# Other rows leave early: the gate's row split at 416, and a last output tile in two steps

## The chip, the cores and the metric

One NeuronCore of a Trainium2 chip. The metric is the device time of one execution in microseconds, the median of three runs. Times within the profile are in us from the start of its span, unless marked ns.

## The reference

Cross-attention with a gate, for 8 batches of 100 query rows (800 rows in all, d = 1024) over 722 memory rows of 512:

```python
memory_proj = einsum('bme,de->bmd', memory, W_mem)
scores = einsum('bnd,bmd->bnm', hidden, memory_proj) / sqrt(D)
memory_context = einsum('bnm,bmd->bnd', softmax(scores), memory_proj)
gate = sigmoid(einsum('bnf,df->bnd', concat([hidden, memory_context]), W_gate) + b_gate)
fused = hidden + gate * memory_context
out = fused * rsqrt(mean(square(fused), -1) + 1e-6) * norm_w
```

All in float32. The kernel keeps the precision by splitting each operand of a large matmul into a high and a low part in float32r and adding three products (high by high, low by high, high by low).

## The kernel before

Everything up to the memory context is done for all 800 rows in the first 217 us and is not touched here. What is left is the half of the gate that comes from the memory context, and the end: gate, fusion, mean of squares, scaling, output. Data lies transposed: a tile t of the output is 128 of the 1024 features on the partitions, with the 800 rows along the free dimension, so one matmul streams rows as columns.

**Steps.** A step (t, r0, r1) of the list `STEPS` (L32) makes output tile t for rows r0 to r1. The rows are parted at `FIRST` = 512 (L20): "early" rows 0 to 511 and "late" rows 512 to 799 (288 of them). The order is written by hand: tiles 0 and 1 early, tile 0 late, tiles 2 to 7 early (the last of these is step `END0` = 8), then tiles 1 to 7 late (steps 9 to 15, `LAST` = 15). Step n uses PSUM bank 4 or 5 in turn (`gate_bank`, L126).

**TensorE.** `gate_mc(n)` (L451) runs 8 tiles of the contraction by 3 products, 24 matmuls (L294) whose moving operand has r1 - r0 columns, each with a weight load of 128 columns. Inside step 10 it makes the means of squares for the early rows (`mean_first`, L466: a matmul with the square sums as weights and one column that holds 1/1024), and inside step 11 it spreads the inverse roots over the partitions (`inverse`, L474: ones times a diagonal matrix).

**ScalarE**, for each step (L707 to L716): the weight split for a later step, `sigmoid(n)` (L675) from PSUM, `seed(n + 2)` (L686), which puts the saved half of the gate into the bank of step n + 2, and `finish(n - 1)` (L696), which is a square and then `weigh` (L691), a scaling by norm_w. At two steps, 9 and 15, finish comes ahead of the sigmoid. For the last step VectorE squares (L932), and ScalarE only weighs (L718).

**VectorE**, for each step: `gate_times` (L877), `fuse` (L883), `sum_squares(n - 1)` (L864), and from step 11 on two scaled outputs of the early rows (`output`, L895). **SyncE** stores the early rows in transposed form, two tiles at a time (L278), as these become ready.

**The late rows leave otherwise**: TensorE transposes them back, in three chunks of `CHUNK` = 96 rows. Behind the last gate step TensorE does, in program order (L500 to L514): the first seven tiles of chunks 0 and 1 turned, a wait for the square sums and the last square, the late means (two matmuls for each chunk, L506 and L507), the last tile of chunks 0 and 1, and all of chunk 2. VectorE adds eps to the three means (L934), GpSimd raises them to -0.5 (L954), and then each chunk is scaled by its roots on its way out of PSUM: ScalarE takes the left half of its 1024 columns (L722), VectorE the right half (L938). SyncE stores a chunk as 96 rows of 4 KB (L282) when both halves are there, and waits for all stores (L284). `TURN` (L23) says which two PSUM banks a chunk is turned into.

Of the kernel before, what the change touches and what calls it, by code (L numbers as in the profile page):

```python
# [7 lines left out]
P = 128  # L8
R = B * N
H = R // 2  # L10
KD, KC = D // P, C // P
# [3 lines left out]
BANK = 512  # L15
WB = KD * P
EPS = 1e-6
WARM_UP = 27

FIRST, CHUNK = 512, 96  # L20
ROWS2 = (R - FIRST) // CHUNK

TURN = ((0, 1), (2, 7), (4, 3))  # L23


J_MEM = 0
# [3 lines left out]


STEPS = [(0, 0, FIRST), (1, 0, FIRST), (0, FIRST, R)] + [(t, 0, FIRST) for t in range(2, KD)] \  # L32
    + [(t, FIRST, R) for t in range(1, KD)]
LAST = len(STEPS) - 1

END0 = STEPS.index((KD - 1, 0, FIRST))
# [5 lines left out]
def build(nc, xT, ctxT, ctxN, w_mem, w_gate_x, w_mem_t, w_gate_mc, b_gate, norm_w, outT, out_rows):  # L42
    F32, F32R = mybir.dt.float32, mybir.dt.float32r
    ALU, ACT, AX = mybir.AluOpType, mybir.ActivationFunctionType, mybir.AxisListType

    top = ExitStack()
    with top:  # L47
        def sb(scope, name, shape, dt=F32):
            return scope.enter_context(nc.sbuf_tensor(name, shape, dt))
# [11 lines left out]
        acc = sb(top, "acc", [P, KD, R])  # L61
# [34 lines left out]
        minus_half = sb(top, "minus_half", [P, FIRST // P])  # L96
        rms = sb(top, "rms", [P, FIRST // P])
        rms_late = sb(top, "rms_late", [CHUNK, ROWS2])
        rms_diag = sb(top, "rms_diag", [P, FIRST // P, P])


        w_hi.append(sb(top, "w_hi2", [P, WB], F32R))
# [11 lines left out]
        def bank(i, cols, rows=P, at=0):  # L114
            return ps[0:rows, i * BANK + at:i * BANK + at + cols]
# [5 lines left out]
        G2B, RIB = 4, 3  # L121

        def late_mean(i, n=1):
            return bank(6, n, CHUNK, 8 + i)

        def gate_bank(n):  # L126
            r0, r1 = STEPS[n][1:]
# [160 lines left out]
        def _(pe):  # L288
# [162 lines left out]
            def gate_mc(n, after=None, work=None):  # L451

                t, r0, r1 = STEPS[n]
                pe.wait_ge(w_lo_done, J_G2 + 1 + t)
                if n >= 2:
                    pe.wait_ge(seeded, n - 1)
                for k in range(KD):
                    if n == 0:
                        pe.wait_ge(mc_lo_done, k + 1)
                    done = three([gate_bank(n)], w_tile(W_HOME[t], k), [(act_hi[:, k, r0:r1], act_lo[:, k, r0:r1])],  # L460
                                 k == 0 and n < 2, k == KD - 1, onto=n >= 2)
                    if k == after:
                        work()
                done.then_inc(gate_made, 1)

            def mean_first():  # L466

                pe.wait_ge(summed, END0 + 1)
                for i in range(FIRST // P):
                    done = nc.tensor.matmul(bank(6, 1, P, i), square_sum[:, i * P:(i + 1) * P], mean_w[:, :],  # L470
                                            start=True, stop=True)
                done.then_inc(mean_made, 1)

            def inverse():  # L474

                pe.wait_ge(diag_done, FIRST // P)
                for i in range(FIRST // P):
                    done = nc.tensor.matmul(bank(RIB, P, P, i * P), ones[:, :], rms_diag[:, i, :],  # L478
                                            start=True, stop=True)
                done.then_inc(inv_made, 1)  # L480

            def late_sums(i):
                at = FIRST + i * CHUNK
                return square_sum[:, at:at + CHUNK]

            def turn(i, t0, t1):

                at = FIRST + i * CHUNK
                for t in range(t0, t1):
                    done = nc.tensor.transpose(bank(TURN[i][t // 4], P, CHUNK, t % 4 * P), acc[:, t, at:at + CHUNK],  # L490
                                               ident[:, :])
                return done
# [4 lines left out]
            gate_mc(END0 + 3, 4, inverse)  # L497
            for n in range(END0 + 4, LAST + 1):
                gate_mc(n)
            pe.wait_ge(weighted, LAST)  # L500
            turn(0, 0, KD - 1)
            turn(1, 0, KD - 1)
            pe.wait_ge(summed, LAST)
            pe.wait_ge(late_squared, 1)
            for i in range(ROWS2):
                nc.tensor.matmul(late_mean(i), late_sums(i), mean_w[:, :], start=True, stop=False)  # L506
                done = nc.tensor.matmul(late_mean(i), square[:, LAST % 2, i * CHUNK:(i + 1) * CHUNK], mean_w[:, :],  # L507
                                        start=False, stop=True)
            done.then_inc(late_mean_made, 1)
            pe.wait_ge(weighted, LAST + 1)  # L510
            turn(0, KD - 1, KD).then_inc(turned, 1)
            turn(1, KD - 1, KD).then_inc(turned, 1)
            pe.wait_ge(out_done, KD)
            turn(2, 0, KD).then_inc(turned, 1)  # L514


# [1 line left out]
        def _(act):  # L518
# [188 lines left out]
            for n in range(LAST + 1):  # L707
                if n in SPLIT_AT:
                    split_gate_w(SPLIT_AT[n])
                if n == END0 + 1 or n == LAST:  # L710
                    finish(n - 1)
                sigmoid(n)
                if n + 2 <= LAST:
                    seed(n + 2)
                if n > 0 and n not in (END0 + 1, LAST):
                    finish(n - 1)  # L716
            act.wait_ge(late_squared, 1)
            weigh(LAST)  # L718
            for i in range(ROWS2):
                act.wait_ge(late_rooted, 1)  # L720
                act.wait_ge(turned, i + 1)
                nc.scalar.activation(row_out[:, i * D:i * D + BANK], bank(TURN[i][0], BANK, CHUNK), ACT.Copy,  # L722
                                     scale=rms_late[:, i:i + 1]).then_inc(row_left, 1)
# [3 lines left out]
        def _(dve):  # L727
# [160 lines left out]

            def diagonals():
                dve.wait_ge(rooted, 1)  # L890
                for i in range(FIRST // P):
                    nc.vector.tensor_scalar(rms_diag[:, i, :], ident[:, :], rms[:, i:i + 1], None,
                                            ALU.mult).then_inc(diag_done, 1)

            def output(k):  # L895
# [15 lines left out]
            gate_times(END0 + 1)  # L911
            fuse(END0 + 1)
            dve.wait_ge(mean_made, 1)
            nc.vector.tensor_scalar(rms[:, :], bank(6, FIRST // P), EPS, None, ALU.add).then_inc(mean_copied, 1)
            diagonals()
            done = 0
            for n in range(END0 + 2, LAST):
# [6 lines left out]
                while done < min(KD, 2 * (n - END0 - 2)):  # L924
                    output(done)
                    done += 1
            sum_squares(LAST - 1)
            gate_times(LAST)
            fuse(LAST)
            part = acc[:, KD - 1, FIRST:R]  # L930
            dve.wait_ge(fused, LAST + 1)
            nc.vector.tensor_tensor(square[:, LAST % 2, 0:R - FIRST], part, part, ALU.mult).then_inc(late_squared, 1)  # L932
            dve.wait_ge(late_mean_made, 1)
            nc.vector.tensor_scalar(rms_late[:, :], late_mean(0, ROWS2), EPS, None, ALU.add).then_inc(mean_copied, 1)  # L934
            for i in range(ROWS2):
                dve.wait_ge(late_rooted, 1)
                dve.wait_ge(turned, i + 1)
                nc.vector.tensor_scalar(row_out[:, i * D + BANK:(i + 1) * D], bank(TURN[i][1], BANK, CHUNK),  # L938
                                        rms_late[:, i:i + 1], None, ALU.mult).then_inc(row_right, 1)


        @block.gpsimd
        def _(pool):
            nc.gpsimd.memset(ident[:, :], 0.0).then_inc(ident_zeroed, 1)
            pool.wait_ge(ident_zeroed, 1)
# [6 lines left out]
            nc.gpsimd.tensor_tensor(rms[:, :], rms[:, :], minus_half[:, :], ALU.pow).then_inc(rooted, 1)  # L952
            pool.wait_ge(mean_copied, 2)
            nc.gpsimd.tensor_tensor(rms_late[:, :], rms_late[:, :], minus_half[0:CHUNK, 0:ROWS2],  # L954
                                    ALU.pow).then_inc(late_rooted, 1)


# [28 lines left out]
```

## Time and profile before

| | |
|---|---|
| median of 3 runs | 303.08 us (302.94 to 303.28) |
| the profiled execution | 303.27 us |
| its span | 301.5 us |
| granted TensorE clock, mean | 0.992 |
| TensorE busy | 97% of the span |
| VectorE, ScalarE busy | 55%, 52% |
| HBM read, written | 42.80 MB, 3.28 MB |

The profile is of one execution. A busy time counts the instructions of an engine from start to end. Matmuls overlap one another, so the pace of a row of matmuls is read from the starts of the first and the last, and not from the length of one. The weight loads (PEld) run beside the matmuls (PE). A chain of waits goes back from the last instruction, at each step to what released it. A line's number is that of the kernel above.

### The profile page before, as it was taken

The numbers are of one execution on the slowest core, as the hardware profiler recorded it, in microseconds if no ns is written. First come the engines' busy times: TensorE is split into PE (matmuls) and PEld (weight loads), VectorE is DVE, ScalarE is ACT, GpSimd is POOL, SyncE is SP. The second block draws the span as 40 slices with busy tenths as digits, with TensorE's granted clock in tenths as the row PEclk, the third lists the DMA queues.
The fourth block names the chain that finished last, engine by engine and source line by source line (L and its number), as shares of the span: only waits on it lengthen the run. The fifth ranks groups of instructions, "written<-read, shape, count | busy, mean of one in ns | idle before, by whom it ended". The sixth has DMA issues, their size and how long they took to land.

```text
span 301.5 us, 4214 instructions
## 1 busy us (share of the span) xinstructions
PE 292.5 (97%) x1647; PEld 272.2 (90%) x1647; DVE 166.5 (55%) x236; ACT 157.4 (52%) x231; POOL 2.6 (1%) x8
## 2 busy tenths in 40 slices
PE   8999999999999999999999999999999999999990
PEld 7999999898999989899898989999988888899980
DVE  2757564557575666756566534432365753444862
ACT  4648246464573836448373616454356845454542
POOL 0000000000000000000000000000000000001000
PEclk9999999999999999999999999999999999999996
DMA  6997291733928367372944011095123400000335
GB/s 208 408 385 244 94 339 56 238 115 111 277 89 316 136 199 262 105 257 102 299 161 150 13 70 40 29 340 236 70 72 136 143 2 0 1 0 2 139 141 157
DMA packets 18351, 46.29 MB, mean 154 GB/s; under 512 B 1520, under 2 KB 2288, under 8 KB 18336
## 3 DMA queue, kind: packets, MB, share of 16 engines
q1 hardware_dynamic: 18336, 46.09, 44.4%
q8 instruction: 10, 0.16, 0.2%
q14 instruction: 5, 0.04, 0.1%
HBM read 42.80 MB, written 3.28 MB: 153 GB/s over the span
## 4 chain that ended last, share of the span: by engine, by line
PE 96%; DMA 1%; DVE 1%; ACT 0%; DVEq 0%; issue 0%; ACTq 0%
PE ps L294 69%; PE ps L406 11%; PE ps L382 11%; PE ps L396 1%; PE ps L413 1%; DMA acc<-xT 1%; PE ps L319 0%; DVEq L47 0%; PE ps L490 0%; PE ps L322 0%; PE ps L325 0%; PE ps L478 0%; PE ps L470 0%; DVE x_again L938 0%; PE ps L506 0%
## 5 line engine op out<-in xcount | busy, mean ns | idle before, releaser
L294 PE MATMUL ps<-act_hi,w_hi 128*128 128x400 f32 (+2 forms) x268 | 79.4, 347 | 0.0
L294 PE MATMUL ps<-act_hi,w_lo 128*128 128x400 f32 (+2 forms) x268 | 78.7, 344 | 0.0
L294 PE MATMUL ps<-act_lo,w_hi 128*128 128x400 f32 (+2 forms) x268 | 78.7, 344 | 0.0
L294 PEld LDWEIGHTS ps<-act_hi,w_hi 128*128 128x128 f32 x268 | 49.2, 188 | 2.9
L294 PEld LDWEIGHTS ps<-act_lo,w_hi 128*128 128x128 f32 x268 | 49.8, 188 | 1.8
L294 PEld LDWEIGHTS ps<-act_hi,w_lo 128*128 128x128 f32 x268 | 49.8, 188 | 1.8
L729 DVE TENSOR_TENSOR w_lo<-w_stage,w_hi 128x1024 fp32r<-128x1024 f32 (+2 forms) x23 | 26.0, 1131 | 23.4 <-ACT w_hi L526 22.2
L729 DVE TENSOR_TENSOR cn_lo<-cn_stage,cn_hi 128x1536 fp32r<-128x1536 f32 (+2 forms) x24 | 28.5, 1217 | 5.2 <-ACT cn_hi L545 5.2
L729 DVE TENSOR_TENSOR ct_lo<-ct_stage,ct_hi 128x1444 fp32r<-128x1444 f32 x16 | 25.8, 1654 | 0.5 <-ACT ct_hi L537 0.5
L526 ACT ACTIVATE w_hi<-w_stage 128x1024 fp32r<-128x1024 f32 x20 | 21.0, 1054 | 7.9 <-PE ps L294 6.1
L621 ACT ACTIVATE pc<-ps,row_inv 100x512 f32<-100x512 f32 x8 | 5.5, 688 | 34.1 <-PE ps L406 34.1
L537 ACT ACTIVATE ct_hi<-ct_stage 128x1444 fp32r<-128x1444 f32 x16 | 21.7, 1409 | 0.0
L382 PE MATMUL ps<-ct_hi,qb_hi 128*100 128x362 f32 x64 | 21.4, 334 | 0.0
L605 ACT ACTIVATE probs<-ps,neg_top 100x722 f32<-100x722 f32 x8 | 6.9, 866 | 27.2 <-DVE neg_top L807 27.2
L382 PE MATMUL ps<-ct_hi,qb_lo 128*100 128x362 f32 x64 | 21.0, 328 | 0.0
L382 PE MATMUL ps<-ct_lo,qb_hi 128*100 128x362 f32 x64 | 21.0, 328 | 0.0
L683 ACT ACTIVATE gate<-ps,bias_t 128x288 f32<-128x288 f32 (+1 forms) x14 | 8.1, 579 | 24.2 <-PE ps L294 24.2
L881 DVE TENSOR_TENSOR gate<-gate,mc 128x512 f32<-128x512 f32 (+1 forms) x16 | 9.2, 573 | 20.0 <-ACT gate L683 20.0
L729 DVE TENSOR_TENSOR act_lo<-mc,act_hi 128x800 fp32r<-128x800 f32 x8 | 7.9, 993 | 20.5 <-ACT mc L654 20.5
L406 PE MATMUL ps<-cn_hi,pt_hi 128*100 128x512 f32 (+1 forms) x48 | 18.9, 394 | 0.0
L406 PE MATMUL ps<-cn_hi,pt_lo 128*100 128x512 f32 (+1 forms) x48 | 18.9, 393 | 0.0
L406 PE MATMUL ps<-cn_lo,pt_hi 128*100 128x512 f32 (+1 forms) x48 | 18.9, 393 | 0.0
(99 smaller groups left out, 447.1 us busy)
## 6 DMA issues: line engine op xcount, KB each, us to landing
ct_stage<-ctxT SPq DMA_DIRECT2D x16, 722.0 KB, 9.2
cn_stage<-ctxN SPq DMA_DIRECT2D x8, 768.0 KB, 5.4
cn_stage<-ctxN SPq DMA_DIRECT2D x8, 512.0 KB
w_stage<-w_gate_x SPq DMA_DIRECT2D x8, 512.0 KB, 7.9
w_stage<-w_gate_mc SPq DMA_DIRECT2D x8, 512.0 KB, 3.6
x_again<-xT SPq DMA_DIRECT2D x1, 3200.0 KB, 13.0
acc<-xT SPq DMA_DIRECT2D x6, 400.0 KB, 7.3
w_stage<-w_mem_t SPq DMA_DIRECT2D x4, 512.0 KB, 5.5
```

The lines of the kernel that those rows point to most:

```text
L294: done = nc.tensor.matmul(o, wgt, stream[h][part], start=first and wgt is wh and part == 0, stop=last and wgt is wl, skip_group_check=onto)
L382: done = nc.tensor.matmul(bank(h, MH + 1, N), lhs[:, k, :], rhs[:, k, at:at + MH + 1], start=k == 0 and part == 0, stop=k == KC - 1 and pa ...
L396: done = nc.tensor.transpose(o, probs[:, t * P:t * P + rows], ident[0:N, 0:N])
L406: done = nc.tensor.matmul(bank(PCB, C, N), lhs[0:rows, t, :], rhs[0:rows, t, :], start=t == 0 and part == 0, stop=t == MT and part == 2)
L413: done = nc.tensor.transpose(bank(PTB5, N, P, c * N), pc[:, c * P:(c + 1) * P], ident[0:N, 0:N])
L526: nc.scalar.activation(w_hi[home][:, :], w_stage[:, slot, :], ACT.Copy).then_inc(w_hi_done, 1)
L537: nc.scalar.activation(ct_hi[:, 2 * s:2 * s + 2, :], ct_stage[:, 2 * s:2 * s + 2, :], ACT.Copy).then_inc(ct_hi_done, 1)
L605: nc.scalar.activation(probs[:, :].rearrange("p (h m) -> p h m", h=2), scores, ACT.Exp, bias=neg_top[:, :], scale=float(D) ** -0.5, accum_ ...
L621: nc.scalar.activation(pc[:, :], bank(PCB, C, N), ACT.Copy, scale=row_inv[:, :]).then_inc(pc_scaled, 1)
L683: nc.scalar.activation(part, part if n < 2 else gate_bank(n), ACT.Sigmoid, bias=bias_t[:, t:t + 1]).then_inc(gate_done, 1)
L729: return nc.vector.tensor_tensor(out, whole, hi.bitcast(F32), ALU.subtract)
L881: nc.vector.tensor_tensor(part, part, mc[:, t, r0:r1], ALU.mult).then_inc(gated, 1)
```

## The change

- The rows are parted at 416: 416 early rows, 384 late ones, in three chunks of 128 rows.
- The last output tile's late rows are two steps: 256 rows (416 to 671, chunks 0 and 1), then 128 (672 to 799, chunk 2). There are 17 steps, and `LAST` is 16.
- The means of chunks 0 and 1 no longer need the last step: TensorE makes them right behind it, from the square sums alone, and VectorE adds eps to them between `gate_times(16)` and `fuse(16)`; GpSimd has a power of its own for them. The mean of chunk 2 comes later and goes to another bank (7).
- TensorE's order behind the last step: means of chunks 0 and 1, all of chunk 0 turned, mean of chunk 2, chunk 1 turned, chunk 2 turned.
- VectorE's order: eps of chunk 2, then the right halves of chunks 0, 1 and 2.
- ScalarE puts the finish ahead of the sigmoid at steps 9, 15 and 16.
- The matrices of the early rows' scaling are 104 by 104, four of them, in place of 128 by 128.

```diff
-FIRST, CHUNK = 512, 96
-ROWS2 = (R - FIRST) // CHUNK
-
-TURN = ((0, 1), (2, 7), (4, 3))
+FIRST, CHUNK = 416, 128
+ROWS2, LATE = (R - FIRST) // CHUNK, R - CHUNK
+FC = FIRST // 4
+
+TURN = ((0, 1), (2, 3), (5, 4))
...
-    + [(t, FIRST, R) for t in range(1, KD)]
+    + [(t, FIRST, R) for t in range(1, KD - 1)] + [(KD - 1, FIRST, LATE), (KD - 1, LATE, R)]
...
         def late_mean(i, n=1):
-            return bank(6, n, CHUNK, 8 + i)
+            return bank(6, n, CHUNK, 8 + i) if i < ROWS2 - 1 else bank(7, n, CHUNK, BANK - 1)
...
             for n in range(END0 + 4, LAST + 1):
                 gate_mc(n)
+            pe.wait_ge(summed, LAST)
+            for i in range(ROWS2 - 1):
+                done = nc.tensor.matmul(late_mean(i), late_sums(i), mean_w[:, :], start=True, stop=True)
+            done.then_inc(late_mean_made, 1)
             pe.wait_ge(weighted, LAST)
-            turn(0, 0, KD - 1)
-            turn(1, 0, KD - 1)
-            pe.wait_ge(summed, LAST)
+            turn(0, 0, KD).then_inc(turned, 1)
             pe.wait_ge(late_squared, 1)
-            for i in range(ROWS2):
-                nc.tensor.matmul(late_mean(i), late_sums(i), mean_w[:, :], start=True, stop=False)
-                done = nc.tensor.matmul(late_mean(i), square[:, LAST % 2, i * CHUNK:(i + 1) * CHUNK], mean_w[:, :],
-                                        start=False, stop=True)
-            done.then_inc(late_mean_made, 1)
+            nc.tensor.matmul(late_mean(ROWS2 - 1), late_sums(ROWS2 - 1), mean_w[:, :], start=True, stop=False)
+            nc.tensor.matmul(late_mean(ROWS2 - 1), square[:, LAST % 2, 0:CHUNK], mean_w[:, :],
+                             start=False, stop=True).then_inc(late_mean_made, 1)
+            pe.wait_ge(out_done, KD)
+            turn(1, 0, KD).then_inc(turned, 1)
             pe.wait_ge(weighted, LAST + 1)
-            turn(0, KD - 1, KD).then_inc(turned, 1)
-            turn(1, KD - 1, KD).then_inc(turned, 1)
-            pe.wait_ge(out_done, KD)
             turn(2, 0, KD).then_inc(turned, 1)
...
-                if n == END0 + 1 or n == LAST:
+                early = n == END0 + 1 or n >= LAST - 1
+                if early:
                     finish(n - 1)
                 sigmoid(n)
...
             for i in range(ROWS2):
-                act.wait_ge(late_rooted, 1)
+                act.wait_ge(late_rooted, 1 + (i == ROWS2 - 1))
...
+            def late_mean_plus_eps(late, at, n):
+                dve.wait_ge(late_mean_made, late + 1)
+                nc.vector.tensor_scalar(rms_late[:, at:at + n], late_mean(at, n), EPS, None,
+                                        ALU.add).then_inc(mean_copied, 1)
+
             gate_times(LAST)
+            late_mean_plus_eps(0, 0, ROWS2 - 1)
             fuse(LAST)
...
-            nc.vector.tensor_scalar(rms_late[:, :], late_mean(0, ROWS2), EPS, None, ALU.add).then_inc(mean_copied, 1)
-            for i in range(ROWS2):
-                dve.wait_ge(late_rooted, 1)
+            def right_half(i):
+                dve.wait_ge(late_rooted, 1 + (i == ROWS2 - 1))
                 dve.wait_ge(turned, i + 1)
...
+            late_mean_plus_eps(1, ROWS2 - 1, 1)
+            for i in range(ROWS2):
+                right_half(i)
...
-            pool.wait_ge(mean_copied, 2)
-            nc.gpsimd.tensor_tensor(rms_late[:, :], rms_late[:, :], minus_half[0:CHUNK, 0:ROWS2],
-                                    ALU.pow).then_inc(late_rooted, 1)
+            for late, at, n in ((0, 0, ROWS2 - 1), (1, ROWS2 - 1, 1)):
+                pool.wait_ge(mean_copied, late + 2)
+                part = rms_late[:, at:at + n]
+                nc.gpsimd.tensor_tensor(part, part, minus_half[0:CHUNK, 0:n], ALU.pow).then_inc(late_rooted, 1)
```

## Rows read from the trace of the kernel before

**Rows 1.** The page, busy us of each engine, share of the span, instructions

```profile
PE 292.5 (97%) x1647; PEld 272.2 (90%) x1647; DVE 166.5 (55%) x236; ACT 157.4 (52%) x231; POOL 2.6 (1%) x8
```

**Rows 2.** Stretches: length, busy us (matmuls) of each engine, clock, DMA share, GB/s

```profile
182.80:217.65 34.85, 34.85 (x196) 34.85 (x194) 13.69 (x17) 17.14 (x22) 0.00 (x0) 1.00 0.41 155
232.11:265.50 33.39, 33.39 (x146) 27.00 (x145) 16.76 (x24) 18.73 (x29) 0.00 (x0) 1.00 0.14 46
276.04:289.77 13.73, 13.73 (x106) 13.72 (x105) 9.82 (x20) 7.81 (x17) 0.00 (x0) 1.00 0.29 115
```

**Rows 3.** The chain of waits that ended last: start, us, what

```profile
275.04 0.89 PE ps L478 x8
...
290.03 0.51 ACT gate L683
...
290.56 0.47 DVE gate L881
...
291.05 0.47 DVE acc L886
...
291.55 0.47 DVE square L932
...
292.15 0.30 PE ps L506 x2
...
293.13 0.17 PE ps L507 x2
293.30 1.15 PE ps L490 x10
```

**Rows 4.** Timeline of the tail: start, us, engine, line, out<-in, count, idle before

```profile
293.34 0.16 DVE L934 TENSOR_SCALAR rms_late<-ps 96x3 f32<-96x3 f32 x1 [1.33 <-PE ps L507]
293.57 0.85 POOL L954 TENSOR_TENSOR rms_late<-rms_late,minus_half 96x3 f32<-96x3 f32 x1 [20.46 <-DVE rms_late L934]
294.46 1.83 ACT L722 ACTIVATE x_again<-ps,rms_late 96x512 f32<-96x512 f32 x3 [1.88 <-PE ps L490]
294.46 2.06 DVE L938 TENSOR_SCALAR x_again<-ps,rms_late 96x512 f32<-96x512 f32 x3 [0.96 <-PE ps L490]
295.29 1.62 SPq L282 DMA_DIRECT2D out_rows<-x_again  x3
```

**Rows 5.** DMA, GB/s in 40 slices of 279 to 294, 294 to 302, 224 to 232

```profile
GB/s 0 0 0 0 0 38 377 404 426 153 0 0 0 0 202 421 382 382 11 0 0 0 38 371 415 421 153 0 0 0 0 202 421 393 371 11 0 44 0 0
...
GB/s 0 0 0 0 0 0 0 0 0 0 143 328 307 184 225 307 307 266 307 307 369 328 307 307 266 287 348 225 205 246 184 82 61 0 0 0 0 0 0 0
...
GB/s 389 369 164 0 0 20 0 0 20 0 41 41 225 184 184 246 246 369 451 389 143 102 41 0 0 0 0 0 0 0 0 0 0 0 0 0 0 0 0 164
```

**Rows 6.** Timeline: the early rows' means, loads and matmuls, inside step 10

```profile
270.66 0.99 PEld L470 LDWEIGHTS ps<-mean_w,square_sum 128*128 128x128 f32 x8
270.79 0.95 PE L470 MATMUL ps<-mean_w,square_sum 128*128 128x1 f32 x8
```

**Rows 7.** Groups by shape, 225 to 302: count, busy us, mean ns, idle before

```profile
L881 DVE TENSOR_TENSOR gate<-gate,mc 128x512 f32<-128x512 f32 x8 | 5.5, 690 | 14.7 <-ACT gate L683 14.7
L693 ACT ACTIVATE acc<-acc,norm_t 128x512 f32<-128x512 f32 x8 | 5.8, 726 | 0.3
L702 ACT ACTIVATE square<-acc 128x512 f32<-128x512 f32 x8 | 4.9, 616 | 0.0
L693 ACT ACTIVATE acc<-acc,norm_t 128x288 f32<-128x288 f32 x8 | 4.3, 538 | 1.7 <-DVE square L932 1.5
L683 ACT ACTIVATE gate<-ps,bias_t 128x512 f32<-128x512 f32 x6 | 4.1, 690 | 14.6 <-PE ps L294 14.6
L683 ACT ACTIVATE gate<-ps,bias_t 128x288 f32<-128x288 f32 x8 | 4.0, 497 | 9.6 <-PE ps L294 9.6
L881 DVE TENSOR_TENSOR gate<-gate,mc 128x288 f32<-128x288 f32 x8 | 3.7, 456 | 5.3 <-ACT gate L683 5.3
L470 PEld LDWEIGHTS ps<-mean_w,square_sum 128*128 128x128 f32 x8 | 1.0, 191 | 0.0
```

More of the change, by code:

```diff
@@ L95, in build @@
         ones = sb(top, "ones", [P, P])
-        minus_half = sb(top, "minus_half", [P, FIRST // P])
-        rms = sb(top, "rms", [P, FIRST // P])
+        minus_half = sb(top, "minus_half", [P, 4])
+        rms = sb(top, "rms", [FC, 4])
         rms_late = sb(top, "rms_late", [CHUNK, ROWS2])
-        rms_diag = sb(top, "rms_diag", [P, FIRST // P, P])
+        rms_diag = sb(top, "rms_diag", [FC, 4, FC])
         w_hi.append(sb(top, "w_hi2", [P, WB], F32R))
@@ L468, in mean_first @@
                 pe.wait_ge(summed, END0 + 1)
-                for i in range(FIRST // P):
-                    done = nc.tensor.matmul(bank(6, 1, P, i), square_sum[:, i * P:(i + 1) * P], mean_w[:, :],
+                for i in range(4):
+                    done = nc.tensor.matmul(bank(6, 1, FC, i), square_sum[:, i * FC:(i + 1) * FC], mean_w[:, :],
                                             start=True, stop=True)
@@ L474, in inverse @@
             def inverse():
-                pe.wait_ge(diag_done, FIRST // P)
-                for i in range(FIRST // P):
-                    done = nc.tensor.matmul(bank(RIB, P, P, i * P), ones[:, :], rms_diag[:, i, :],
+                pe.wait_ge(diag_done, 4)
+                for i in range(4):
+                    done = nc.tensor.matmul(bank(RIB, FC, P, i * FC), ones[0:FC, :], rms_diag[:, i, :],
                                             start=True, stop=True)
@@ L714, in _ @@
                     seed(n + 2)
-                if n > 0 and n not in (END0 + 1, LAST):
+                if n > 0 and not early:
                     finish(n - 1)
@@ L890, in diagonals @@
                 dve.wait_ge(rooted, 1)
-                for i in range(FIRST // P):
-                    nc.vector.tensor_scalar(rms_diag[:, i, :], ident[:, :], rms[:, i:i + 1], None,
+                for i in range(4):
+                    nc.vector.tensor_scalar(rms_diag[:, i, :], ident[0:FC, 0:FC], rms[:, i:i + 1], None,
                                             ALU.mult).then_inc(diag_done, 1)
@@ L913, in _ @@
             dve.wait_ge(mean_made, 1)
-            nc.vector.tensor_scalar(rms[:, :], bank(6, FIRST // P), EPS, None, ALU.add).then_inc(mean_copied, 1)
+            nc.vector.tensor_scalar(rms[:, :], bank(6, 4, FC), EPS, None, ALU.add).then_inc(mean_copied, 1)
             diagonals()
@@ L927, in _ @@
             sum_squares(LAST - 1)
+            def late_mean_plus_eps(late, at, n):
+                dve.wait_ge(late_mean_made, late + 1)
+                nc.vector.tensor_scalar(rms_late[:, at:at + n], late_mean(at, n), EPS, None,
+                                        ALU.add).then_inc(mean_copied, 1)
             gate_times(LAST)
+            late_mean_plus_eps(0, 0, ROWS2 - 1)
             fuse(LAST)
-            part = acc[:, KD - 1, FIRST:R]
+            part = acc[:, KD - 1, LATE:R]
             dve.wait_ge(fused, LAST + 1)
-            nc.vector.tensor_tensor(square[:, LAST % 2, 0:R - FIRST], part, part, ALU.mult).then_inc(late_squared, 1)
-            dve.wait_ge(late_mean_made, 1)
-            nc.vector.tensor_scalar(rms_late[:, :], late_mean(0, ROWS2), EPS, None, ALU.add).then_inc(mean_copied, 1)
-            for i in range(ROWS2):
-                dve.wait_ge(late_rooted, 1)
+            nc.vector.tensor_tensor(square[:, LAST % 2, 0:CHUNK], part, part, ALU.mult).then_inc(late_squared, 1)
+            def right_half(i):
+                dve.wait_ge(late_rooted, 1 + (i == ROWS2 - 1))
                 dve.wait_ge(turned, i + 1)
@@ L951, in _ @@
             pool.wait_ge(mean_copied, 1)
-            nc.gpsimd.tensor_tensor(rms[:, :], rms[:, :], minus_half[:, :], ALU.pow).then_inc(rooted, 1)
-            pool.wait_ge(mean_copied, 2)
-            nc.gpsimd.tensor_tensor(rms_late[:, :], rms_late[:, :], minus_half[0:CHUNK, 0:ROWS2],
-                                    ALU.pow).then_inc(late_rooted, 1)
+            nc.gpsimd.tensor_tensor(rms[:, :], rms[:, :], minus_half[0:FC, :], ALU.pow).then_inc(rooted, 1)
+            for late, at, n in ((0, 0, ROWS2 - 1), (1, ROWS2 - 1, 1)):
+                pool.wait_ge(mean_copied, late + 2)
+                part = rms_late[:, at:at + n]
+                nc.gpsimd.tensor_tensor(part, part, minus_half[0:CHUNK, 0:n], ALU.pow).then_inc(late_rooted, 1)
 def kernel(x, ctx_1024, L0_xattn_W_mem, L0_xattn_W_gate, L0_xattn_b_gate, L0_xattn_norm_w):
```

## The prediction

> **What bounds the kernel now.** I read the page's busy line first: TensorE is busy for 292.5 of 301.5 us [rows 1], so a change to the work beside it is worth nothing until the last matmul is out. The chain of waits, read from its end, says what follows. The last gate matmul is issued at 289.77 [rows 2] and the sigmoid of the last step starts at 290.03, 0.26 later; from there one step of 288 rows goes through ScalarE and VectorE piece by piece, 0.5 us each (sigmoid, times, fuse, square), until TensorE takes the means at 292.15 and the last transposes at 293.30 [rows 3]. The timeline of the tail shows the rest [rows 4]: VectorE adds eps, GpSimd takes the power in 0.85, both halves of a chunk are evicted, and three stores of 384 KB are issued from 295.29 on, the last at 296.6. The view of the DMAs gives the end: nothing moves before about 296.1 (0.8 after the first issue), the three stores then run into one another until about 300.4, and the span ends at 301.5, 1.1 later [rows 5]. So three things in series set the end: the TensorE stream, the chain after its last step, and a store queue that is full once the first chunk is out. The end is the first store's issue plus 6.2 us.
>
> The profiled execution took 303.27, 1.77 more than its span; the median of the runs is 303.08, 0.19 lower. I work in the span and convert at the end. A difference under 0.2% (0.6 us) can't be told from none.
>
> **TensorE's stream.** Rows are only parted differently (416 and 384 in place of 512 and 288), so for seven of the eight tiles the question is whether the pace per product is linear in columns. 144 products of 512 columns took 33.39, 0.2319 each; 103 of 288 took 13.73, 0.1333 each [rows 2]. The line through them gives 0.1826 at 400, where 192 products took 34.85 us, 0.1815 each [rows 2]. It holds, and gives 0.1896 at 416 and 0.1756 at 384, together 0.3652, the same as now. Those seven tiles cost nothing.
>
> The last tile becomes 416, 256 and 128. At 256 the line gives 0.1192. At 128 the trace has no such product, and I bound it. From below: the line, 0.063. From above: the plain float32 products of 128 columns in the row scaling, eight records of 0.111 for four products in 0.89 us, 0.222 a product [rows 3]. Between them lies the weight load: eight loads of 128 columns with only one column streamed after each took 0.99 [rows 6]; one alone lasts 0.19 [rows 7], so they came at (0.99 - 0.19) / 7 = 0.114 each. All matmuls of 288 columns and more hide such a load, one of 128 can't. I take 0.113. The tile then costs 24 x (0.1896 + 0.1192 + 0.113 - 0.3652) = 1.36 us more. The eight loads of the means and the eight of the scaling shrink from 128 to 104 columns, which gives back some 0.2 (96 columns load at 0.17 / 2 = 0.085 in the late means [rows 3]). Net +1.16: the last gate matmul is issued at 290.93, step 15 ends at 288.22, step 14 at 285.36.
>
> The Trainium skill, "TensorE: Matmul & The Clock Gate", section "Back-to-back issue gap", gives some 81 ns per matmul at 128 columns for a stream of load and matmul pairs; no product here shows it. By it the step would cost 0.77 less than by my value.
>
> **The work beside it.** Early steps shrink to 4.55 us of TensorE each, and ScalarE's and VectorE's parts shrink with the columns; the heaviest early step there (a weight split and four passes) stays below that, so no step turns over. Late steps grow to 4.2 us, with more room for the scaled outputs. The mean and the scaling matmuls sit four tiles into steps 10 and 11 and have more time than now. The four output stores are 416 KB, the last is issued near 289 and is through before 292: off the path. The seam is steps 14 to 16, where ScalarE now does two finishes between sigmoids. Between 512 and 288 columns sigmoid and weighting scale at about 0.85 ns a column [rows 7], and I take the square with them from its 0.62 at 512: sigmoid 0.58, square 0.51, weighting 0.62 at 384; 0.47, 0.41, 0.51 at 256; 0.36 for the sigmoid at 128. Sigmoid 14 starts at 285.62; it, a seed (0.3), and the finishes of 13 and 14 take 3.1, less some overlap, so sigmoid 15 starts at 288.6, some 0.1 late. VectorE's two passes at 256 take 0.42 each (1.04 ns a column from 0.69 and 0.46 [rows 7]), then square and weighting: ScalarE is free at 290.9, and sigmoid 16 can start with its matmuls at 291.19. Cover 0.3.
>
> **The chain after the last step** has 128 columns in place of 288: sigmoid 0.36, times, fuse and square 0.29 each. One thing is put in it: VectorE adds eps for chunks 0 and 1 (0.16) between times and fuse; its means were issued right after the stream, so it waits for nothing, and GpSimd's power for them ends near 292.9. The square ends at 292.66 instead of 292.02, 0.64 later for a stream 1.16 later. TensorE had 12 mean records between the square and the eps; it has 4 now, so chunk 2's eps starts 0.6 us after TensorE's start at 292.80, at 293.4, where it was 1.19 after. Meanwhile chunk 0 has been transposed (eight at 0.115 [rows 3]), but its right half is queued on VectorE behind that eps: 293.58 to 294.32 at 0.74 [rows 4]. The weighting of step 16 and the left half fit beside it on ScalarE. **First store at 294.41, 0.88 earlier than now.** The transposes of chunk 1 start at 293.2 and of chunk 2 at 294.1, 0.92 each; with 0.25 until VectorE sees them and 0.74 for the half, stores go out at 295.25 and 296.15. The second power (0.85 from 293.6) is done before chunk 2 wants it.
>
> **The stores.** Each is 512 KB in place of 384, 1.57 MB in place of 1.18. Now 384 KB takes a third of 4.3 us, 1.43, at plateaus near 307 GB/s from 96 partitions in pieces of 4 KB; the output stores move 512 KB from 128 partitions in pieces of 2 KB at plateaus near 400, in 1.3 [rows 5]. What makes the difference, partitions or piece? The weight loads have 128 partitions and 4 KB pieces and reach 369 to 451 GB/s for some slices [rows 5]. That speaks for the partitions. I take 1.3 a store: 3.9, from 294.41 + 0.8 = 295.2 to 299.1, the later issues being in time. With 1.1 after it the span ends at 300.2, 1.3 less than now: 301.97, as a median **301.8 us**. Bounds: 4.3 x 4/3 = 5.7 for the three if pieces decide, below.
>
> The Trainium skill, "SBUF — State Buffer", section "Door 1: The DMA port swizzle", says that partitions 0 to 63 all sit on half of the 16 ports. By it 96 partitions leave the even ports as much to carry as 128 do, and a store of 512 KB would take as long as one of 384 KB. The 307 against 400 fits.
>
> **Rivals.**
> - *The small product is cheap.* At the line's 0.063 the stream ends 1.2 earlier, but ScalarE is busy with step 15 until 290.9: only the cover of 0.3 is gained, 301.5 us. For it: the loads overlap the longer matmuls. Against: the pace of 0.114 [rows 6]. Chance 0.10. The figure of the Trainium skill's page above would end at the same 301.5, for the same cover.
> - *A product of 128 columns goes at the plain float32 price* (0.222): 24 x 0.109 = 2.6 us more, all ahead of every chunk, because the means of chunks 0 and 1 are issued behind the step. 304.4 us, **slower**. It decides from 0.166 a product on (no gain left) and makes it slower by over 0.6 us from 0.19. For it: the only 128-column products there are cost that. Against: they are two records each, a gate product is one. Chance 0.12.
> - *Pieces of 4 KB set the store rate.* 295.2 + 5.7 + 1.1 = 302.0, 303.8 and as a median 303.6 us: the tail gives back all that the chain won. Chance 0.13.
> - *Chunk 0 leaves no earlier*, because ScalarE's two finishes run late and sigmoid 16 with them, or VectorE's queue is held by the second eps: the stores then win only their 0.4. 302.7 us. Chance 0.07.
>
> **How the numbers follow.** My forecast has 0.58: 301.8, alone 301.0 to 302.4. The range of 300.9 to 303.6 takes in the first, third and fourth rival and leaves out the plain price and the edges. Faster by over 0.6 us: my forecast and the cheap product but for their upper edge, 0.64; the same: the third and fourth mostly, 0.19; slower: the plain price and a part of the third, 0.17.
>
> **What would show it.** The 24 products of the last step at 0.113 spacing (0.06 or 0.22 for the rivals); sigmoid 16 at 0.26 after the stream, with ScalarE idle before it; first eps between times and fuse; first store near 294.4 and the last near 296.2; plateaus near 400 GB/s under 512 KB stores, and 5.8 us from first issue to the end. I am wrong if the step takes over 4 us, if ScalarE has no gap before sigmoid 16, or if the stores still move at 300 GB/s.

## The result, and the profile after

Over four runs each the changed kernel took 300.51 us (300.26 to 300.65), the kernel before 303.02 (302.94 to 303.28): a ratio of 0.9916, 95% interval 0.9904 to 0.9928, which is 2.5 us less. Repeated twice beside further runs of the kernel before it came out at 0.9927 (0.9914 to 0.9941) and 0.9922 (0.9909 to 0.9936), medians of 300.68 both times against 302.79 and 302.94: 2.1 and 2.3 us. The forecast was 301.8 us, a gain of 1.3, with a range from 300.9. The direction and the mechanism were right, the size was too small, and the time lies below the range: the term for TensorE's stream was 0.58 us too large, the one for the chain behind it 0.25.

The page of the changed kernel, busy us and share of a span of 298.9 (compare [rows 1]):

```profile
PE 292.9 (98%) x1667; PEld 280.5 (94%) x1667; DVE 166.3 (56%) x240; ACT 158.8 (53%) x235; POOL 3.0 (1%) x9
```

TensorE's busy time has grown by 0.4 us and the span has shrunk by 2.6: what went was time without matmuls.

The stretches of the gate stream, with length, then busy us and instructions of each engine, clock, DMA share, GB/s. In order they are 48 products of 416 columns, 144 of 416, 39 of 384, 24 of 256, and 21 of the 24 of 128 (compare [rows 2]; a stretch also counts the one or two matmuls that reach into it):

```profile
217.30:226.32 9.02, 9.02 (x49) 8.97 (x49) 4.99 (x6) 5.66 (x7) 0.00 (x0) 1.00 0.36 101
230.49:257.67 27.18, 27.18 (x145) 26.95 (x145) 14.83 (x22) 16.23 (x27) 0.00 (x0) 1.00 0.15 45
257.67:264.46 6.79, 6.79 (x40) 6.79 (x40) 3.40 (x6) 4.38 (x8) 0.00 (x0) 1.00 0.00 0
284.55:287.38 2.83, 2.83 (x25) 2.83 (x25) 1.92 (x4) 2.47 (x6) 0.00 (x0) 1.00 0.42 156
287.55:289.89 2.34, 2.34 (x23) 2.34 (x23) 1.99 (x5) 1.36 (x4) 0.00 (x0) 1.00 0.40 154
```

The paces are 0.1888 us at 416, 0.1741 at 384, 0.1179 at 256 and 2.34 / 21 = 0.111 at 128. The last one is close to the 0.113 that the prediction took for the weight load. The other three are all a little below the line through 288 and 512.

The chain that ended last, from TensorE's stream on: start, us, what (compare [rows 3]):

```profile
279.98 10.19 PE ps L295 x75
290.17 0.03 issue
290.20 0.61 PE ps L503 x4
290.80 0.93 PE ps L491 x8
291.73 0.31 PE ps L508 x2
292.05 0.22 PE ps L509 x2
292.27 1.82 PE ps L491 x16
...
294.19 0.75 DVE x_again L944
```

The four passes of the last step are no longer on the chain. TensorE goes from the stream into the means, the transposes of chunk 0, the last mean (L508, L509) and the other 16 transposes, and the last step's passes run beside chunk 0's. The timeline of the other engines in the same stretch (compare [rows 4]):

```profile
289.62 0.51 ACT L693 ACTIVATE acc<-acc,norm_t 128x256 f32<-128x256 f32 x1
290.19 0.52 PEld L503 LDWEIGHTS ps<-mean_w,square_sum 128*128 128x128 f32 x4 [0.17 <-DVE square_sum L870]
290.27 0.37 ACT L683 ACTIVATE gate<-ps,bias_t 128x128 f32<-128x128 f32 x1
290.87 0.15 DVE L931 TENSOR_SCALAR rms_late<-ps 128x2 f32<-128x2 f32 x1
291.11 0.74 POOL L966 TENSOR_TENSOR rms_late<-rms_late,minus_half 128x2 f32<-128x2 f32 x1 [24.45 <-DVE rms_late L931]
291.32 0.29 DVE L939 TENSOR_TENSOR square<-acc 128x128 f32<-128x128 f32 x1
...
292.31 0.16 DVE L931 TENSOR_SCALAR rms_late<-ps 128x1 f32<-128x1 f32 x1 [0.70 <-PE ps L509]
292.39 0.75 DVE L944 TENSOR_SCALAR x_again<-ps,rms_late 128x512 f32<-128x512 f32 x1
...
293.23 2.11 SPq L283 DMA_DIRECT2D out_rows<-x_again  x3
```

The first store goes out at 293.23, 2.06 earlier than at 295.29; 0.35 of that is only that this execution reached the gate earlier (217.30 against 217.65). What the stores then take is shown by the GB/s in 40 slices of 291.3 to 299 (compare the second line of [rows 5]):

```profile
GB/s 0 0 0 0 0 0 0 0 0 0 0 0 0 0 298 362 447 404 362 468 362 447 404 362 404 426 383 404 405 404 426 404 468 362 170 0 0 0 0 0
```

1.57 MB moves at about 400 GB/s in 3.9 us, where 1.18 MB took 4.3.

### The profile page after: what moved, and what is told of

Read it like the earlier page. It is cut to its first block, busy times and chain, and to the rows that moved or that the text cites. A ratio compares the mean times of both kernels' runs of the same rounds, so it can differ in the third digit from the quotient of the medians.

```text
span 298.9 us, 4266 instructions
## 1 busy us (share of the span) xinstructions
PE 292.9 (98%) x1667; PEld 280.5 (94%) x1667; DVE 166.3 (56%) x240; ACT 158.8 (53%) x235; POOL 3.0 (1%) x9
## 4 chain that ended last, share of the span: by engine, by line
PE 97%; DMA 1%; ACT 0%; DVE 0%; issue 0%; DVEq 0%
PE ps L295 70%; PE ps L407 11%; PE ps L383 11%; PE ps L397 1%; PE ps L414 1%; PE ps L491 1%; DMA acc<-xT 1%; PE ps L320 0%; PE ps L479 0%; PE ps L323 0%; DVE x_again L944 0%; PE ps L326 0%; PE ps L471 0%; PE ps L503 0%; ACT act_hi L553 0%; PE ps L508 0%
## 5 line engine op out<-in xcount | busy, mean ns | idle before, releaser
L295 PE MATMUL ps<-act_hi,w_hi 128*128 128x400 f32 (+4 forms) x276 | 81.0, 343 | 0.0
L295 PE MATMUL ps<-act_hi,w_lo 128*128 128x400 f32 (+4 forms) x276 | 80.4, 340 | 0.0
L295 PE MATMUL ps<-act_lo,w_hi 128*128 128x400 f32 (+4 forms) x276 | 80.2, 340 | 0.0
L295 PEld LDWEIGHTS ps<-act_hi,w_hi 128*128 128x128 f32 x276 | 50.7, 188 | 1.3 <-DVE act_lo L730 0.3
L295 PEld LDWEIGHTS ps<-act_lo,w_hi 128*128 128x128 f32 x276 | 51.3, 188 | 0.1
L295 PEld LDWEIGHTS ps<-act_hi,w_lo 128*128 128x128 f32 x276 | 51.3, 188 | 0.0
L683 ACT ACTIVATE gate<-ps,bias_t 128x384 f32<-128x384 f32 (+3 forms) x15 | 8.5, 570 | 24.7 <-PE ps L295 24.5
L882 DVE TENSOR_TENSOR gate<-gate,mc 128x416 f32<-128x416 f32 (+3 forms) x17 | 9.4, 550 | 21.1 <-ACT gate L683 20.9
```

The costliest lines, as they stand in the source:

```text
L295: done = nc.tensor.matmul(o, wgt, stream[h][part], start=first and wgt is wh and part == 0, stop=last and wgt is wl, skip_group_check=onto)
L683: nc.scalar.activation(part, part if n < 2 else gate_bank(n), ACT.Sigmoid, bias=bias_t[:, t:t + 1]).then_inc(gate_done, 1)
```

## A sum in three parts

Up to the gate the kernels are the same, and all traces of this study can be read by three lengths: from the first gate matmul to the first matmul behind the gate (stream), from there to the issue of the first row store (chain), and from there to the end of the span (tail). All are in us.

| kernel | stream | chain | tail | sum against before | measured, medians |
|---|---|---|---|---|---|
| before | 72.12 | 5.52 | 6.21 | | |
| changed | 72.90 | 3.03 | 5.67 | -2.25 | -2.5, -2.1, -2.3 |
| e1: parting at 416 alone | 71.40 | 6.38 | 5.64 | -0.43 | -0.47 |
| e2: two steps alone | 74.22 | 2.98 | 5.92 | -0.73 | -0.60 |
| e3: half rows stored | 72.12 | 5.40 | 5.87 | -0.46 | -0.37 |
| e4: 464, chunks of 112 | 73.27 | 3.11 | 6.67 | -0.80 | -0.68 |
| e5: half 0 ahead | 72.89 | 2.53 | 5.79 | -2.64 | -2.64 |
| e9: half 1 too | 72.89 | 2.53 | 5.64 | -2.79 | -2.85 |

Each sum agrees with the difference of the medians on one chip to within some 0.26 us. The changed kernel's stream holds 0.2 of waiting: its last gate matmul started at 289.89, the next matmul could have followed near 290.0, and the means were held until 290.20 by a square sum (the PEld row above).

## The experiments

**Parting at 416 alone.** From the kernel before:

```diff
-FIRST, CHUNK = 512, 96
+FIRST, CHUNK = 416, 128
 ROWS2 = (R - FIRST) // CHUNK
+FC = FIRST // 4
...
```

and the early rows' scaling in four blocks of 104, as in the change.

> The parting at 416 and the chunks of 128 rows alone; the last tile is one step of 384 rows and the order behind it is that of the kernel before. Theory: (a) products of 384 and 416 columns cost 0.174 and 0.189 us, a little under the line through 288 and 512 (0.1756, 0.1896), because those of 512 carry some 4 ns more than their columns, so the stream ends 0.7 to 0.9 earlier than before; (b) the chain behind it is 0.45 longer (384 columns in place of 288); (c) a store of 128 rows takes the 1.3 us that one of 96 takes. First store at 294.8, end of the span near 300.5, median 302.1 us. Rival, the shorter stream of the changed kernel is an accident of its run: the paces are the line's, the median is 302.8. Rival, stores go by bytes: first issue to end 7 us and more, the median is 303.5.

Measured: 302.42 us, ratio 0.9982 (0.9972 to 0.9992). The stretches of 48 and of 144 products of 416 columns:

```profile
216.98:226.00 9.02, 9.02 (x50) 8.98 (x49) 4.99 (x6) 5.66 (x7) 0.00 (x0) 1.00 0.30 105
230.16:257.34 27.18, 27.18 (x145) 26.95 (x145) 14.81 (x22) 16.22 (x27) 0.00 (x0) 1.00 0.14 48
```

They repeat the changed kernel's to the hundredth, so the low pace is no accident, and the stream is 0.72 shorter than before, as expected. The tail is 5.64, as expected. The chain came out 0.86 longer where 0.45 was expected. The sigmoid and the three passes behind it account for 0.38. The twelve mean matmuls behind the square took 1.63 us up to the eps instead of 1.19, for two reasons. They load 128 columns each and not 96, and their pairs start 0.22 apart instead of 0.17. And the clock fell under the last pair: clock (the third number from the end) ahead of it and behind it, then the last two L508 pairs:

```profile
291.00:292.20 1.20, 1.05 (x10) 1.08 (x10) 0.00 (x0) 0.61 (x1) 0.00 (x0) 1.00 0.00 0
292.40:292.60 0.20, 0.20 (x2) 0.20 (x3) 0.00 (x0) 0.00 (x0) 0.00 (x0) 0.50 0.00 0
291.81 0.36 PE L508 MATMUL ps<-mean_w,square 128*128 128x1 f32 x2
292.25 0.49 PE L508 MATMUL ps<-mean_w,square 128*128 128x1 f32 x2
```

The granted clock went from 1.00 to 0.50, TensorE's lower level (1.2 GHz of 2.4), after TensorE had waited 1.07 us for the square. From the start of the last pair to the eps it took 0.53 here and 0.40 in the changed kernel, whose clock was still 1.00. So some 0.13 of the 0.44 belongs to the clock of this execution and not to the parting.

The first store's time of 294.76 fits the forecast only because this trace's stream also began 0.67 earlier (see e7).

**Two steps alone.** From the changed kernel:

```diff
-FIRST, CHUNK = 416, 128
+FIRST, CHUNK = 512, 96
```

> The parting at 512 and chunks of 96 rows kept, but the last tile in two steps (192 and 96 rows) and the changed order behind it. Theory: a product that streams less than its weight load takes costs the load, 0.112 us, for 192 columns and for 96 alike; the two steps cost 24 x (0.112 + 0.112 - 0.134) = 2.1 us more than the one of 288. The first store goes out 3.1 after the stream, near 295.0, the stores take 6.2 to the end as before: median 302.8 us. Rival, small products go by their columns (0.091 and 0.049): stream as before, ScalarE holds the last sigmoid, median 301.0.

Measured: 302.29 us, ratio 0.9977 (0.9967 to 0.9987). The 24 products of 192 columns, then 23 of those of 96:

```profile
286.40:289.06 2.66, 2.66 (x26) 2.66 (x25) 1.94 (x6) 2.30 (x6) 0.00 (x0) 1.00 0.54 203
289.17:291.70 2.53, 2.53 (x26) 2.53 (x24) 1.98 (x5) 1.36 (x4) 0.00 (x0) 1.00 0.44 172
```

2.66 / 24 = 0.111 and 2.53 / 23 = 0.110: twice the columns at the same price. The floor goes with the load and not with the product: the pairs of mean matmuls of e1 stream one column each and start 0.11 a matmul apart behind loads of 128 columns, and 0.084 behind the loads of 96 in the kernel before [rows 3]. The rival of a cheap small product is gone. The stream grew by 2.1, as expected, and the chain fell by 2.5. The gain was 0.6 and not 0.1, mostly because the third part moved too: the stores here go out 0.88 apart in place of 0.65 and the tail is 5.92, where I had kept 6.2. Why stores further apart end sooner was not tried.

**Half rows stored.** From the kernel before:

```diff
-                sp.wait_ge(row_left, i + 1)
-                sp.wait_ge(row_right, i + 1)
-                sp.dma_start(out_rows[i * CHUNK:(i + 1) * CHUNK, :],
-                             row_out[:, i * D:(i + 1) * D]).then_inc(stored, 16)
+                for h, ready in enumerate((row_left, row_right)):
+                    sp.wait_ge(ready, i + 1)
+                    sp.dma_start(out_rows[i * CHUNK:(i + 1) * CHUNK, h * BANK:(h + 1) * BANK],
+                                 row_out[:, i * D + h * BANK:i * D + (h + 1) * BANK]).then_inc(stored, 16)
...
```

> The kernel before, each chunk of 96 rows stored as two stores of 96 partitions with pieces of 2 KB in place of one with pieces of 4 KB. Theory, the partitions set the rate: plateaus stay near 300 GB/s, 4.0 to 4.3 us of moving, the end as before or 0.1 to 0.2 earlier from the earlier first issue, median 302.9 us. Rival, the pieces set the rate: plateaus near 400 as in the output stores of 2 KB pieces, 3.0 us of moving, median 301.8.

Measured: 302.52 us, ratio 0.9986 (0.9977 to 0.9996). GB/s in slices of 0.2 us, 294 to 302:

```profile
GB/s 0 0 0 0 0 0 0 61 256 236 307 318 297 297 348 287 358 287 338 307 266 348 318 348 297 266 205 113 31 10 0 0 0 0 0 0 0 0 0 0
```

Pieces of 2 KB from 96 partitions go at about 300 GB/s, as those of 4 KB did, while 128 partitions reach 400 with either. The partitions set the rate, not the pieces; the third rival has fallen. The small gain is 0.12 less of chain and 0.34 less of tail.

One more difference could stand behind the 300 and the 400: under the stores of the kernel before TensorE's granted clock was 0.50 from 297 on, under those of the changed kernel it was 1.00. The stores of e1 settle it. The changed kernel's, then e1's (clock, DMA share, GB/s at the end):

```profile
294.10:298.00 3.90, 0.00 (x0) 0.00 (x0) 0.75 (x1) 0.69 (x1) 0.00 (x0) 1.00 0.99 397
295.60:299.60 4.00, 0.00 (x0) 0.00 (x0) 0.39 (x1) 0.17 (x1) 0.00 (x0) 0.50 0.98 392
```

128 partitions move 392 GB/s at the lower clock as well.

**Parting at 464, chunks of 112.** From the changed kernel:

```diff
-FIRST, CHUNK = 416, 128
+FIRST, CHUNK = 464, 112
```

> The changed kernel with the parting at 464 and chunks of 112 rows; the last tile in 224 and 112 rows. Theory: 464 columns 0.21, 336 columns 0.154, both small steps at the load's 0.112, stream 0.45 later than in the changed kernel; the stores of 448 KB from 112 partitions take the same 1.3 us each as 512 KB from 128 (plateaus near 350 GB/s), first issue to end 5.7. Median 300.9 to 301.0 us. Rival, stores go at 400 GB/s for any bytes from many partitions: 0.3 to 0.4 less. Rival, the load sets no floor at 224 columns: 0.104 a product, 0.2 less.

Measured: 302.21 us, ratio 0.9976 (0.9966 to 0.9985), 1.2 more than the theory gave and still more than its rivals did. The stream was 72.90 + 0.37, near the expected 0.45; 24 products of 224 columns and 23 of 112 again go at the floor, 0.111 and 0.110:

```profile
285.32:287.99 2.67, 2.67 (x26) 2.67 (x25) 1.80 (x4) 2.31 (x6) 0.00 (x0) 1.00 0.49 184
288.10:290.62 2.52, 2.52 (x25) 2.52 (x24) 2.21 (x6) 1.53 (x4) 0.00 (x0) 1.00 0.38 150
```

The miss is all in the stores. GB/s in slices of 0.21 us, 292 to 300.4:

```profile
GB/s 0 0 0 0 0 0 0 0 0 0 0 0 293 273 332 234 312 312 254 371 234 312 293 293 332 293 312 312 254 293 371 293 254 176 98 59 0 0 0 0
```

1.38 MB takes 4.8 us, at a plateau of about 293 GB/s. A store from 112 partitions takes 1.6 us, one from 96 takes 1.43, and one from 128, with more bytes than either, 1.3. Of these three partition counts only the full 128 reaches 400 GB/s. By the rule of the Trainium skill ("SBUF — State Buffer", "Door 1: The DMA port swizzle") the busiest port has as many partitions behind it at 112 as at 128; an estimate by that rule is that 112 partitions take the same 1.3. The measurement decides against it here. What in the spread over engines and ports makes 112 partitions slow was not tried.

**Right half of chunk 0 ahead of the last eps.** From the changed kernel:

```diff
+            right_half(0)
             late_mean_plus_eps(1, ROWS2 - 1, 1)
-            for i in range(ROWS2):
+            for i in range(1, ROWS2):
                 right_half(i)
```

> The changed kernel with VectorE's right half of chunk 0 ahead of the eps of chunk 2. Theory: that half waits for nothing but its place in the queue (it could start near 291.95 and starts at 292.39), and the three stores run into one another, so the first issue sets the end: first store 0.4 earlier, the span 0.3 to 0.45 shorter than the changed kernel's, median 300.1 us; the eps of chunk 2, 0.4 later, is still in time for its power. Rival, the last store's own issue (295.0, set by the transposes of chunk 2) sets the end: no difference, median 300.5.

> The kernel of e5 once more, beside the changed kernel and e9 on one chip. Theory: 0.3 to 0.45 under the changed kernel. Rival, no difference: the 0.5 between the medians of the last call was the spread of the runs.

Measured: 300.15 us beside 300.68 of the changed kernel, and 300.41 beside 300.68 in the repeat; ratios to the kernel before of 0.991 (0.9895 to 0.9925) and 0.9911 (0.9897 to 0.9924), against 0.9927 and 0.9922. The intervals overlap, so the medians alone don't settle it, but both pairs point the same way and the chain is 2.53 in both traces against 3.03 to 3.04 in the three of the changed kernel. VectorE and the store queue:

```profile
291.77 0.75 DVE L944 TENSOR_SCALAR x_again<-ps,rms_late 128x512 f32<-128x512 f32 x1 [0.28 <-POOL rms_late L967]
292.44 0.15 DVE L931 TENSOR_SCALAR rms_late<-ps 128x1 f32<-128x1 f32 x1
292.61 2.62 SPq L283 DMA_DIRECT2D out_rows<-x_again  x3
```

Only the power holds the half now. The first store goes out 0.5 earlier and the end 0.4 earlier by the table. Not all of the 0.5 arrives, since the queue runs dry before the second store: in GB/s from 291 to 299, slices of 0.2, one sees the dip of 205 and 287.

```profile
GB/s 0 0 0 0 0 0 0 0 0 0 0 0 307 451 389 430 369 471 205 287 348 492 369 410 369 471 369 410 389 451 369 389 123 0 0 0 0 0 0 0
```

**Chunk 1 early too.** From e5, TensorE turns chunk 1 ahead of chunk 2's mean, and VectorE evicts both right halves ahead of the last eps:

```diff
-            pe.wait_ge(late_squared, 1)
-            ...
             pe.wait_ge(out_done, KD)
             turn(1, 0, KD).then_inc(turned, 1)
+            pe.wait_ge(late_squared, 1)
+            ...
```

> The kernel of e5 with chunk 1 early as well: TensorE turns chunk 1 ahead of chunk 2's mean, and VectorE evicts the right halves of chunks 0 and 1 ahead of chunk 2's eps. Theory: in e5 the store queue runs dry for some 0.3 between the first two stores, since chunk 1 was turned behind chunk 2's mean; here the second store goes out near 293.5 and the three run into one another again, so the end moves by that 0.3, to where the last store's own issue (295.0) sets it: span 298.1, median 299.9 us. Rival, chunk 2 is later by as much as chunk 1 is earlier (its mean, eps and power move back by 0.9), and nothing is won or 0.2 lost: median 300.2 to 300.4.

> The changed kernel once more, as what e9 and e10 are compared with. Theory: 2.1 to 2.3 under the kernel before, 0.3 to 0.45 over e10.

Measured: 300.09 us (299.61 to 300.27), ratio 0.9901 (0.9886 to 0.9916), beside 300.41 of e5 and 300.68 of the changed kernel: the fastest version here, 2.85 under the kernel before, and between the theory's 299.9 and the rival's 300.2. The dip is gone (GB/s from 291 to 299), and what comes last is now chunk 2, which waits for its power (the 0.67):

```profile
GB/s 0 0 0 0 0 0 0 0 0 0 0 0 0 471 389 410 348 471 410 389 369 471 369 410 369 389 451 389 430 471 348 451 62 0 0 0 0 0 0 0
...
293.65 0.55 POOL L967 TENSOR_TENSOR rms_late<-rms_late,minus_half 128x1 f32<-128x1 f32 x1 [1.76 <-DVE rms_late L931]
294.23 0.75 DVE L944 TENSOR_SCALAR x_again<-ps,rms_late 128x512 f32<-128x512 f32 x1 [0.67 <-POOL rms_late L967]
```

By the sum of the traces the step from e5 is 0.15, by the medians 0.3; the intervals can't tell it from none.

**Finish behind sigmoid 15.** From the changed kernel:

```diff
-                early = n == END0 + 1 or n >= LAST - 1
+                early = n == END0 + 1 or n == LAST
```

> The changed kernel, but at step 15 ScalarE's finish comes behind the sigmoid as in most steps; only step 16 has it ahead. Theory: the two finishes take the same time in either order, sigmoid 15 starts 0.13 earlier and finish 15 has to wait for finish 14 instead: free before sigmoid 16 either way, median within 0.1 us of the changed kernel's. Rival, ScalarE is what holds sigmoid 16: 0.2 to 0.5 later or earlier.

Measured: 300.69 us, ratio 0.9931 (0.9916 to 0.9946), the changed kernel beside it 300.68. ScalarE's row before the last step:

```profile
289.81 0.37 ACT L683 ACTIVATE gate<-ps,bias_t 128x128 f32<-128x128 f32 x1 [0.24 <-PE ps L295]
```

It stood idle for 0.24 and waited for the matmuls. ScalarE does not hold sigmoid 16 in either order, so the early finish at step 15 is worth nothing. The one at step 16 was not tried alone.

**The two kernels once more.**

> The kernel before once more, for its trace. Theory: the gate stream starts anywhere between 216.9 and 217.7, by how late the clock is granted among the first matmuls, and takes 72.1 us; the first store goes out 5.5 after it. Rival, the 0.35 by which it starts earlier in the changed kernel belongs to the change: it starts at 217.6 again.

> The changed kernel once more, beside the others on one chip. Theory: its sums are 0.6 more of stream, 2.3 less from the stream to the first store, 0.5 less from there to the end: 2.2 under the kernel before on the same chip, median 300.6 us. Rival, some of the first difference of 2.5 was the spread of four runs: 1.5 to 1.9.

Measured: the kernel before 302.59 (one run, span 300.8), its stream from 216.97, 72.11 long, chain 5.54; the changed kernel 300.68 (ratio 0.9927), its stream from 217.17. So the start of the stream is the run's, not the change's, and the gain of 2.1 lies at the theory's 2.2 and above the rival's 1.5 to 1.9. The chain of the profile on which the prediction rested, at the kernel's first matmuls:

```profile
5.34 0.67 PE ps L322 x2
6.00 0.67 PE ps L325 x2
6.67 0.42 PE ps L319 x2
```

and of the repeat:

```profile
5.15 0.37 PE ps L322 x2
5.52 0.36 PE ps L325 x2
5.88 0.36 PE ps L319 x2
```

A pair of matmuls of 400 columns, 800 in all, takes 0.67 us in one and 0.36 in the other, 1.2 and 2.2 columns a ns, which fits TensorE's two clocks of 1.2 and 2.4 GHz. That it is the clock is read from the pace alone: the granted clock of this stretch reads 1.00 in the profile. In the first execution two such pairs more and a part of a third went at the slow pace, 0.67 us together, where its stream began 0.68 later.

## Why the prediction was wrong in size

**What bounds the kernel** was read rightly: stream, chain and a store queue that is full from the first issue. e5 moved the first issue alone, and the end followed it until the queue ran dry.

**The stream** was to grow by 1.16 from 72.12 and grew by 0.58 (289.89 + 0.11 - 217.30 = 72.70; the prediction's 289.77 is likewise where the next matmul starts, not the last gate matmul, which started at 289.63). The step that failed is "for seven of the eight tiles the question is whether the pace per product is linear", answered with the line through 288 and 512 and "Those seven tiles cost nothing". It is not linear at its upper end. Over its columns at 2.4 GHz a product costs 13 ns more at 288, 14 at 336 and 384, 15 to 16 at 416, 17 at 464 and 19 at 512 (e4 for 336 and 464). The row of 400 columns, 0.1815 where the line gives 0.1826, had shown it, and I wrote "It holds". I had also ended the stretch of 512 columns too early: the first product of 288 starts at 265.57 and not at 265.50, so that 144 products took 0.2323 each.

```profile
265.57 0.29 PE L294 MATMUL ps<-act_hi,w_hi 128*128 128x288 f32 x1
```

Summed over all their products, the 192 early ones took 8.50 less than before where the line gives 8.12, and the 168 late ones of the seven tiles 6.96 more where it gives 7.11. That is 0.53 us on a term put at nothing. e1 shows it apart from all else: of the 0.72 by which its stream is shorter 0.58 are products, where the line gives nothing. The last tile took 0.12 less than its terms (0.1179 in place of 0.1192, and 2.62 for the 24 of 128 columns in place of 2.71). The narrower loads gave back 0.14 and not 0.2, because only those of the means shrank. The scaling matmuls load the matrix of ones, which keeps its 128 columns, and took 0.81 as before:

```profile
L479 PEld LDWEIGHTS ps<-rms_diag,ones 104*128 104x128 f32 x8 | 1.0, 191 | 0.0
L471 PEld LDWEIGHTS ps<-mean_w,square_sum 128*104 128x104 f32 x8 | 0.9, 171 | 0.0
```

**The price of 128 columns**, the disputed term, was right: 0.113 taken, 0.111 measured, and e2 and e4 show the same at 96, 112, 192 and 224. Neither the plain float32 price (0.12 of chance) nor a cheaper product, at the line's 0.063 or at 0.081, happened.

**The chain** was to be 3.48 from the last gate matmul to the first store and was 3.23. Its order was as forecast, and the half of chunk 0 did queue behind the second eps; that alone costs 0.5 (e5). The passes from the sigmoid to the end of the square took 1.34 and not 1.47, the mean followed the square by 0.06 and not 0.14, and the half of chunk 0 followed the start of the eps by 0.08 and not 0.18. The lengths were right, 1.39 added up in both; I had put gaps between them, where VectorE starts the eps 0.09 before the end of the pass ahead of it. The mean itself took 0.64 and not 0.6. ScalarE was free ahead of sigmoid 16 as forecast, though by less, 0.14 and not 0.3: free at 290.13, sigmoid 16 at 290.27. I had not seen that the means would wait for the square sum of step 15, which cost TensorE 0.2 but not the end of the square.

**The stores** were to take 5.8 from first issue to end and took 5.67, at the forecast 1.3 each. The choice of partitions over pieces was right (e3); the reason that I gave beside it, ports, does not carry to 112 partitions (e4), and it made a store from 96 partitions as long as one from 128, where they took 1.43 and 1.3.

These three make 0.58 + 0.25 + 0.13 = 0.96 us, which is what the prediction missed: a forecast gain of 1.3 and one of 2.25 by the traces. The rest of the first result's 2.5 is no more than the spread of the runs, since the repeats gave 2.1 and 2.3. The range was drawn for dearer outcomes and reached only 0.9 below the forecast, and all three terms erred to the same side. None of the signs of being wrong came up: every one of them stood for a slower kernel.

**The two parts of the change need each other.** Alone they win 0.43 and 0.73 by the traces, together 2.25. Two steps at 96 rows a chunk put both on the floor of the load (24 x (0.111 + 0.110 - 0.134) = 2.1 us), while with 384 late rows only the smaller one is on it (24 x (0.118 + 0.111 - 0.174) = 1.3). The parting alone also widens the passes behind the last gate matmul and leaves all twelve mean matmuls, grown to 128 columns, behind the last square, where the two steps leave 128 columns in the passes and four mean matmuls. By the table the 1.09 us that they win together beyond the two gains added up is 0.60 of stream (0.8 less the wait of 0.2) and 0.81 of chain, less 0.32 of tail, since either change alone already shortens the tail. Some 0.13 of the chain's share is the fallen clock of e1's trace.

## What to carry to other kernels

When a tail is a chain that fills a store queue, the first store's issue time and the time of one store are what counts: look for what is queued ahead of the first chunk's eviction, and, where the chunks can be cut so, store from all 128 partitions, the fastest of the three counts measured here. Splitting the last step to shorten the chain costs the weight load for every product narrower than the load, so widen the step until one half is above it. And a line through two measured sizes should be checked against every third size in the trace, to the last digit, if it is to be multiplied by hundreds.

## What the runs showed of the hardware

- Stores of rows from 96 and 112 partitions moved at about 300 GB/s, from 128 at 400 (392 with the granted clock at 0.50, 397 at 1.00), so that a store of 512 KB (1.3 us) is faster than one of 384 (1.43) or 448 KB (1.6). Pieces of 2 or 4 KB made no difference.
- A float32r product with its own weight load of 128 columns takes 0.110 to 0.111 us at 96, 112, 128, 192 and 224 columns, and 0.118 at 256.
- At a granted clock of 1.00 products of 512 columns cost 19 ns over their columns at 2.4 GHz (0.232 us), those of 384 only 14 (0.174).
- In e1 the granted clock fell from 1.00 to 0.50 between 292.20 and 292.40, after TensorE had waited 1.07 us, and the last pair of mean matmuls ahead of the eps took 0.13 longer.
- The first matmuls of 400 columns change from a pace of 0.67 us a pair to 0.36 at a time that differs between executions, which moved everything behind it by up to 0.7 us; an execution's own start has to be taken out before two traces are compared.
